# Moving the input normalisation of an attention and feed-forward kernel from VectorE to ScalarE and GpSimd, with a new instruction order on all engines

## The chip, the cores and the metric

The kernel runs on one core of one Trainium2 chip, in one launch. The metric is device time in microseconds (us). A core has engines that run side by side, each with its own in-order instruction stream: TensorE (PE in the profile), VectorE (DVE), ScalarE (ACT), GpSimd (POOL) and SyncE (SP), which here only issues DMA transfers. They wait for each other through semaphores.

## The reference, cut to what matters

The input is 16 sequences of 512 rows by 256 columns. Attention has 16 heads of 16 columns; its softmax is a second-order polynomial, so that sums over keys can be taken once per sequence. A layer normalisation stands ahead of attention, another behind it, and the same around a feed-forward product whose input and weight are rounded to a six-bit grid in blocks of 32.

```python
def _layernorm(x, axis=-1, eps=1e-05):
    m = jnp.mean(x, axis=axis, keepdims=True)
    v = jnp.var(x, axis=axis, keepdims=True)
    return (x - m) / jnp.sqrt(v + eps)

# inside attention
h = (x - mu) * jax.lax.rsqrt(var + EPS) * ln_w + ln_b
q = h @ w_q
kv = h @ w_kv
# heads, rotary embedding, then
def _taylor_softmax(x):
    t = 1.0 + x + 0.5 * x * x
    return t / jnp.sum(t, axis=-1, keepdims=True)

x = x + _layernorm(attention(_layernorm(x)))
x = x + _layernorm(ffn(_layernorm(x)))
```

The change touches the first normalisation, `(x - mean) * rstd`, whose result is named `z`.

## The kernel before

The 16 x 512 rows are 64 tiles of 128 rows, four tiles per sequence. Every tile goes through the same stages, and the tiles overlap deeply: while tile 30 is being normalised, the projections of tile 28, the attention of tile 21 or 22 and the feed-forward product of tile 13 are under way. The polynomial softmax makes attention two phases: `sum_features` adds up products of keys and values over the four tiles of a sequence (features `kf`, values `vp`, into the banks `ps_mt`), then, per quad of heads, `select` and `attend` apply these sums to the queries.

For each tile, in short:

- VectorE: `stats_x`, `moments_x` (mean and variance, `mv`), `normalise_x` (writes `z`), after the transpose `low_h` (`hT_l`), after the projection `rope_sin`, `rope_cos`, `rope_add` (rotary embedding into `kf`), `extend_k`, `products_0` and `products_1` (feature products), `normalise_attention` (`att`), `add_attention` (`xs`), and the quantisation and closing steps of the feed-forward part (`amax`, `sc`, `inv`, `y`, `xd`, `xdT_l`, `fb`, `fin`).
- GpSimd: `add_x` and `rstd_x` (the inverse root `rs_x` of the variance, by a power), the same pair for the three other normalisations, `half_turn`, `products_2`, `low_q`, `low_attention`.
- TensorE: `turn_z` (transposes `z` into `ps_tr`), `project_kq` (six products of 512 columns into `ps_qk`), `project_v` (six of 256 into `ps_tr`), `turn_q`, five `select` products of 512 columns into `ps_f`, `attend` (eight products of 32 output rows and 512 columns), `sum_features` (16 of 153 columns), `project_out` and `ffn` (six of 256 each, into `ps_w`) and `turn_ffn_input`.
- ScalarE: `high_h` (`hT_h`, the high part of the transposed `z`), `square` five times (from `ps_f` into `feat`), `copy_quad` (`osb`), `copy_q`, `copy_v`, `high_q`, `square_k`, `centre`, the three squares for the variances, and further copies out of the accumulation banks.

The bank `ps_tr` serves `turn_z`, `turn_ffn_input`, `project_v` and `turn_q` one after the other; each waits until ScalarE, or ScalarE and then VectorE, has read what the last one left. So `turn_z`, `high_h`, `low_h` is a chain across three engines that closes before the next use.

The order of the work on each engine is a table of numbers, `ORDER`: for each stage, the slots at which its tiles stand in the engine's stream (a list of first slots, a cycle of four tiles with a pitch, and a list of last slots). `every_step` walks through the slots and emits the stage that stands there. `IDLE` names slots at which TensorE runs products whose result nobody reads (`idle_products`, two per entry `fill`; `warm_up` is twelve of them at the start). In the kernel before, `IDLE` is empty.

The normalisation that is moved, in the kernel before (line 1476 and on):

```python
def normalise_x(t):
    dve.wait_ge(rstd["x"], t.n)
    wait(dve, zT_done, t.n - 2)
    dve.tensor_scalar(z[:, t.two, 0:D - 1], xa[:, t.par, t.tile, 0:D - 1], mv[:, t.two, 0:1], rs["x"][:, t.two:t.two + 1],
                      ALU.subtract, ALU.mult).then_inc(z_ready, 1)
```

At the start of the program, before tiles can flow, the projection weights are folded with the layer norm's weights (`fold_kq`, `fold_v` on TensorE), split into a high and a low part (`wkqv_h` on ScalarE, `wkqv_l` on VectorE), and VectorE and ScalarE work out the angles of the rotary embedding and the rounding of the feed-forward weight.

Of the kernel before, what the change touches and what calls it, by code (L numbers as in the profile page):

```python
# [6 lines left out]
ALU = mybir.AluOpType  # L7
# [6 lines left out]
P = 128  # L14
D = 256
# [35 lines left out]
        "attend": ((43, 54, 65, 76, 90, 101, 114, 127, 140, 154, 168, 183, 198,), (25, 39, 53, 69,), (474, 489, 503,  # L51
            517, 533, 547, 561, 574, 591, 605, 619, 632, 643, 662, 676, 690, 706, 720, 734, 748, 763, 778, 791, 807,
            822, 841, 852, 863, 871, 884, 895, 911, 921,)),
        "ffn": ((143, 157, 173, 187, 204,), (145, 159, 173, 189,), (464, 480, 494, 508, 522, 539, 553, 565, 581, 597,
            611, 625, 640, 656, 670, 684, 698, 714, 727, 742, 757, 772, 787, 799, 813, 829, 842, 855, 872, 877, 885,
            896, 906, 913, 922, 928, 934, 937, 940, 943, 945, 947,)),
        "fold_kq": ((2,), (), ()),
        "fold_v": ((3,), (), ()),
        "project_kq": ((4, 8, 12, 17, 22, 28, 39, 50, 61, 73, 86, 97, 110, 122, 136, 150, 164, 176,), (-69, -55, -39,
            -25,), (526, 541, 555, 568, 584, 599, 613, 627, 637, 653, 667, 681, 695, 711, 729, 741, 754, 768, 785, 800,  # L60
            814, 830, 846,)),
        "project_out": ((108, 120, 132, 148, 161, 178, 194, 211, 225, 240, 255, 267, 281, 298, 311, 327, 341, 354,
            369,), (109, 124, 139, 153,), (531, 545, 559, 572, 589, 603, 617, 631, 648, 660, 674, 688, 701, 718, 731,
            746, 762, 776, 792, 804, 820, 834, 848, 859, 866, 880, 889, 900, 910, 918, 923, 929, 933, 936, 941,)),
        "project_v": ((5, 7, 13, 18, 23, 26, 37, 49, 62, 71, 84, 96, 107, 118, 135, 149, 163, 174, 188, 203, 215, 229,
            245,), (-74, -60, -44, -30,), (493, 507, 521, 537, 551, 567, 580, 595, 609, 623, 638, 654, 669, 683, 696,
            712, 724, 739, 752, 771, 784, 798, 815, 831, 847,)),
        "rest_matrix": ((29, 75, 128, 185, 242, 300,), (9,), (527, 585, 644, 705, 764, 821, 876,)),
# [1764 lines left out]
```

## Time and profile before

| | |
|---|---|
| time, median of 3 runs | 645.48 us (644.69 to 649.01) |
| time of the profiled execution | 651.11 us |
| its span, first to last instruction | 648.8 us |
| busy: TensorE | 615.9 us, 95% |
| busy: VectorE | 594.8 us, 92% |
| busy: ScalarE | 530.0 us, 82% |
| busy: GpSimd | 449.3 us, 69% |
| mean granted TensorE clock | 0.985 |

The profile comes from one execution. Its page gives busy time by engine, the costliest groups of instructions (line, engine, output <- input, count, busy time, mean duration, idle time just before them), and what ended the waits. A timeline lists instructions in order of time; equal neighbours are merged into one row. A matmul's end is modelled and overlaps the start of the next one, so that a busy TensorE need not be TensorE at its peak; the distance from one start to the next tells more. A matmul on 32-bit data is recorded as two, so "x8" is four such products. The other engines too show instructions that overlap by about a tenth of a microsecond when they follow directly.

### The profile page before, as it was taken

To read this page: it belongs to the slowest core of one execution; us is meant where nothing else is said; L and a number is where in the kernel's file an instruction comes from. 1 tells how busy PE (TensorE), PEld (TensorE's weight loads), DVE (VectorE), ACT (ScalarE), POOL (GpSimd) and SP (SyncE) were. 2 spreads that over 40 slices of the span, in tenths; PEclk is the share of its full clock that TensorE was granted. 3 is DMA by queue.
4 is the path that set the end of the run, shared out by engine and by line. 5 is a ranking of instruction groups with operands and counts; after the bars stand their busy time and mean duration, and the time that the engine had idled before them with its cause. 6 is when DMAs were issued, how large, how long until landed. Compare 5 with 4: busy or idle time off the path is not lost. (4 is left out here: it accounts for less than half of the span.)

```text
span 648.8 us, 20724 instructions
## 1 busy us (share of the span) xinstructions
PE 615.9 (95%) x6620; PEld 457.7 (71%) x6620; DVE 594.8 (92%) x1489; ACT 530.0 (82%) x1448; POOL 449.3 (69%) x785
## 2 busy tenths in 40 slices
PE   6889999999999999999999999999999999999974
PEld 5666667676776776777777777767777766788763
DVE  5799899899899989999999999989999999987796
ACT  4347788888788897989888888978888888999973
POOL 3475466677777878788777867767877777765464
PEclk9699999999999999999999999999999999999996
DMA  7101031222223232232323232223223212230201
GB/s 245 34 2 42 20 76 30 72 63 65 50 72 88 70 91 68 75 84 67 62 67 83 77 86 73 69 57 101 60 68 92 76 39 41 68 91 18 68 26 49
DMA packets 52362, 43.51 MB, mean 67 GB/s; under 512 B 7201, under 2 KB 48545, under 8 KB 52257
## 3 DMA queue, kind: packets, MB, share of 16 engines
q1 hardware_dynamic: 51440, 41.42, 24.1%
q8 instruction: 55, 0.90, 0.6%
q10 hardware_dynamic: 816, 0.79, 0.4%
q14 instruction: 51, 0.41, 0.2%
HBM read 18.65 MB, written 8.39 MB: 42 GB/s over the span
## 5 line engine op out<-in xcount | busy, mean ns | idle before, releaser
L1168 ACT ACTIVATE feat<-ps_f 128x512 f32<-128x512 f32 x256 | 144.4, 599 | 4.9 <-PE ps_f L852 4.3
L691 DVE TENSOR_TENSOR kf<-kf 128x896 f32<-128x896 f32 (+1 forms) x128 | 131.2, 1027 | 1.8
L852 PE MATMUL ps_f<-qT,selr 128*128 128x512 f32 x320 | 122.1, 435 | 1.8 <-ACT qT L1236 1.3
L691 POOL TENSOR_TENSOR kf<-kf 128x224 f32<-128x224 f32 x64 | 76.5, 1195 | 13.3 <-DVE kf L1515 11.1
L1015 PEld LDWEIGHTS ps_mt<-kf,vp 128*32 128x32 f32 x2048 | 64.1, 110 | 30.0 <-issue 28.3
L1015 PE MATMUL ps_mt<-kf,vp 128*32 128x153 f32 x2048 | 79.7, 296 | 0.6 <-DVE kf L691 0.6
L1725 POOL TENSOR_TENSOR qsp<-kf,qsp 128x256 fp32r<-128x256 f32 x64 | 58.6, 916 | 9.8 <-ACT qsp L1259 9.6
L852 PEld LDWEIGHTS ps_f<-qT,selr 128*128 128x128 f32 x320 | 52.8, 190 | 15.2 <-issue 11.0
L913 PE MATMUL ps_o<-feat,main 120*32 120x512 f32 x448 | 59.7, 604 | 0.0
L916 PE MATMUL ps_o<-feat,rm 128*32 128x512 f32 x448 | 58.6, 593 | 0.0
L788 PE MATMUL ps_qk<-wkqv_h,hT_l 128*128 128x512 f32 x128 | 52.4, 409 | 3.3 <-DVE wkqv_l L1425 3.3
L1737 POOL TENSOR_TENSOR kf<-kf 128x128 f32<-128x128 f32 x64 | 37.4, 584 | 25.9 <-DVE kf L1508 25.8
L1750 POOL TENSOR_TENSOR ve_x<-mv,epsx 128x1 f32<-128x1 f32 x64 | 22.9, 358 | 45.5 <-DVE mv L1474 44.5
L1253 ACT ACTIVATE osb<-ps_o,cb 128x512 f32<-128x512 f32 x56 | 38.5, 687 | 15.9 <-PE ps_o L916 15.0
L789 PE MATMUL ps_qk<-wkqv_l,hT_h 128*128 128x512 f32 x128 | 51.0, 399 | 0.0
L1744 POOL TENSOR_TENSOR attT_l<-att,attT_h 128x256 fp32r<-128x256 f32 x56 | 42.7, 763 | 11.7 <-ACT attT_h L1208 10.9
L1236 ACT ACTIVATE qT<-ps_tr 128x512 fp32r<-128x512 f32 x64 | 38.2, 596 | 14.1 <-PE ps_tr L876 13.3
L1499 DVE TENSOR_TENSOR t<-ps_qk,sinT 128x512 f32<-128x512 f32 x64 | 43.4, 678 | 5.1 <-PE ps_qk L791 4.8
L1750 POOL TENSOR_TENSOR ve_s<-var_s,epst 128x1 f32<-128x1 f32 x64 | 21.8, 341 | 37.4 <-issue 32.4
L1170 ACT ACTIVATE feat<-ps_f,small 128x512 f32<-128x512 f32 x64 | 44.3, 692 | 2.7 <-PE ps_f L852 1.1
L1490 DVE TENSOR_TENSOR t<-ps_qk,cosT 128x512 f32<-128x512 f32 x64 | 43.1, 674 | 2.0 <-PE ps_qk L791 1.6
L1754 POOL TENSOR_TENSOR rs_x<-ve_x,mhalf 128x1 f32<-128x1 f32 x64 | 43.3, 676 | 2.4
(199 smaller groups left out, 1885.2 us busy)
## 6 DMA issues: line engine op xcount, KB each, us to landing
xc<-L_attn_x SPq DMA_DIRECT2D x16, 512.0 KB, 4.5
result<-fin SPq DMA_DIRECT2D x64, 128.0 KB, 2.0
xa<-L_attn_x SPq DMA_DIRECT2D x15, 512.0 KB, 4.1
heads_out<-osb SPq DMA_DIRECT2D x224, 32.0 KB, 2.0
shares<-sums SPq DMA_DIRECT2D x112, 64.0 KB
sums<-osb SPq DMA_DIRECT2D x224, 2.0 KB
wkqv<-L_attn_w_kv ACTq DMA_DIRECT2D x2, 256.0 KB, 4.9
xa<-L_attn_x SPq DMA_DIRECT2D x1, 384.0 KB, 6.2
```

What stands on the lines that cost most here:

```text
L691: return eng.tensor_tensor(dims(row, F_MAIN, [[FW, heads], [HD, NR - 1], [1, HD]]), dims(row, F_LIN, [[FW, heads], [0, NR - 1], [1, HD]]), ...
L788: pe.matmul(out_, xl(c), wh(c), start=c == 0, stop=False)
L789: pe.matmul(out_, xh(c), wl(c), start=False, stop=False)
L852: pe.matmul(ps_f[i % 2][:, :], selr[:, i], queries, start=True, stop=True).then_inc(sel_done, 1)
L913: pe.matmul(ps_o[VW * h:VW * (h + 1), :], main[0:NP, par, quad, VW * h:VW * (h + 1)], feat[0:NP, p2, h], start=True, stop=False, skip_grou ...
L916: mm = pe.matmul(ps_o[VW * h:VW * (h + 1), :], rm[:, par, quad, VW * h:VW * (h + 1)], feat[:, p2, HQ], start=False, stop=True, skip_group_ ...
L1015: mm = pe.matmul(ps_mt[qd // 2][VW * h:VW * (h + 1), (qd % 2) * NF:(qd % 2 + 1) * NF], vp[:, s2, qd * HQ + h], kf[:, s2, qd * HQ + h, 0:NF ...
L1168: act.activation(feat[:, p2, i], ps_f[i % 2][:, :], ACT.Square).then_inc(squared, 1)
L1170: act.activation(feat[:, p2, i], ps_f[0][:, :], ACT.Square, bias=rest_add).then_inc(squared, 1)
L1499: dve.tensor_tensor(dims(t2[:], 0, [[HD, 2 * H], [2, 8], [1, 2]]), dims(ps_qk[:, :], 1, [[HD, 2 * H], [2, 8], [-1, 2]]), sin, ALU.mult).th ...
L1725: pool.tensor_tensor(dims(qsp[:, p2], HQ * HD, [[2 * HQ * HD, NQ], [HD, HQ], [1, HD]]), dims(kf[:, p2, 0, 0:1], F_Q, [[HQ * FW, NQ], [FW, ...
L1750: pool.tensor_tensor(ve[c][:, t.two:t.two + 1], variance, floor, ALU.add).then_inc(pool_step[c], 1)
```

## The change

The normalised input is no longer written by VectorE as `(x - mean) * rstd`, but by ScalarE as `x * rstd + shift`, where `shift = -mean * rstd` is one number per row, worked out by GpSimd in a new step `shift_x` (tile `centre_x`). Two waits guard the double-buffered small tiles: `rstd_x` and `shift_x` wait until ScalarE has written `z` two tiles back, and `moments_x` until the shift two tiles back is there. `constant` and `rest_terms`, once per sequence, are each cut into two stages with the same instructions, which the order may place apart. All slots of `ORDER` are new, and `IDLE["fill"]` has twelve entries, so 24 products whose result nobody reads are added to the first 20 slots of TensorE.

```diff
-IDLE = {"fill": (), "drain": ()}
+IDLE = {"fill": (1, 1, 4, 4, 4, 7, 9, 10, 14, 14, 19, 19,), "drain": ()}
...
+        centre_x = sb("centre_x", [P, 2])
...
+            def normalise_x(t):
+                act.wait_ge(x_centred, t.n)
+                wait(act, zT_done, t.n - 2)
+                act.activation(z[:, t.two, 0:D - 1], xa[:, t.par, t.tile, 0:D - 1], ACT.Identity,
+                               bias=centre_x[:, t.two:t.two + 1], scale=rs["x"][:, t.two:t.two + 1]).then_inc(z_ready, 1)
...
             def moments_x(t):
                 dve.wait_ge(stats, t.n)
                 wait(dve, z_ready, t.n - 2)
+                wait(dve, x_centred, t.n - 2)
                 dve.bn_aggr(mv[:, t.two], st[:, t.two]).then_inc(means, 1)
-
-            def normalise_x(t):
-                dve.wait_ge(rstd["x"], t.n)
-                wait(dve, zT_done, t.n - 2)
-                dve.tensor_scalar(z[:, t.two, 0:D - 1], xa[:, t.par, t.tile, 0:D - 1], mv[:, t.two, 0:1], rs["x"][:, t.two:t.two + 1],
-                                  ALU.subtract, ALU.mult).then_inc(z_ready, 1)
...
+            def sum_linear(t):
+
+                dve.wait_ge(mt_copied, t.seq + 1)
+                wait(dve, cb_ready, t.seq)
+                dve.tensor_reduce(lins[:], mts[:, :, F_LIN:NF], AX.X, ALU.add).then_inc(lins_done, 1)
+
             def constant(t):
-
-                dve.wait_ge(mt_copied, t.seq + 1)
-                dve.tensor_reduce(lins[:], mts[:, :, F_LIN:NF], AX.X, ALU.add).then_inc(lins_done, 1)
                 dve.wait_ge(lins_done, t.seq + 1)
...
             def rstd_x(t):
+                wait(pool, z_ready, t.n - 2)
                 inverse_root("x", t)
+
+            def shift_x(t):
+
+                pool.wait_ge(rstd["x"], t.n)
+                wait(pool, z_ready, t.n - 2)
+                pool.tensor_scalar(centre_x[:, t.two:t.two + 1], mv[:, t.two, 0:1], rs["x"][:, t.two:t.two + 1], -1.0,
+                                   ALU.mult, ALU.mult).then_inc(x_centred, 1)
```

VectorE, in the middle of the program, behind `low_h` of the 29th tile. Before:

```order
L1575 TENSOR_TENSOR hT_l<-ps_tr,hT_h 128x256
L1604 TENSOR_SCALAR sc<-amax 128x8
L1499 TENSOR_TENSOR t<-ps_qk,sinT 128x512
L1608 RECIPROCAL inv<-sc 128x8
L1612 SCALAR_TENSOR_TENSOR y<-c,inv 128x256
L1582 TENSOR_TENSOR xdT_l<-ps_tr,xdT_h 128x256
L1479 TENSOR_SCALAR z<-xa,mv,rs_x 128x255
L1593 SCALAR_TENSOR_TENSOR xs,ssum<-ps_w,rs_y,xc 128x256
L1620 SCALAR_TENSOR_TENSOR xd<-y,rs_s,sc 128x256
L1508 TENSOR_TENSOR kf<-t 128x2x16x16
```

And now, behind the same instruction:

```order
L1586 TENSOR_TENSOR hT_l<-ps_tr,hT_h 128x256
L1521 COPY kf<-kf 128x16x7
L696 TENSOR_TENSOR kf<-kf 128x6x112
L1604 SCALAR_TENSOR_TENSOR xs,ssum<-ps_w,rs_y,xc 128x256
L696 TENSOR_TENSOR kf<-kf 128x8x112
L1593 TENSOR_TENSOR xdT_l<-ps_tr,xdT_h 128x256
L1610 TENSOR_REDUCE amax<-c 128x8
L1481 BN_STATS st<-xa 128x6
L1569 TENSOR_TENSOR att<-heads_out,shares 128x256
L1505 TENSOR_TENSOR t<-ps_qk,sinT 128x512
```

The instruction that wrote `z` is gone, and the feature products now stand directly behind `low_h`, with the rotary embedding later.

ScalarE, in the same round, now (the row that writes `z` is new; `feat` are the squares, `ps_f` their input, `qT` is `copy_q`):

```order
L1173 ACTIVATE feat<-ps_f 128x512 x2
L1232 ACTIVATE vp<-ps_tr 128x16x16
L1175 ACTIVATE feat<-ps_f,small 128x512
L1218 ACTIVATE z<-xa,centre_x,rs_x 128x255
L1247 ACTIVATE qT<-ps_tr 128x4x128
L1213 ACTIVATE attT_h<-att 128x256
L1173 ACTIVATE feat<-ps_f 128x512
```

The same place before:

```order
L1168 ACTIVATE feat<-ps_f 128x512
L1170 ACTIVATE feat<-ps_f,small 128x512
L1236 ACTIVATE qT<-ps_tr 128x4x128
L1208 ACTIVATE attT_h<-att 128x256
L1216 ACTIVATE hT_h<-ps_tr 128x256
```

Behind the new instruction stand `copy_q`, the high part of attention and the first square of the next quad.

TensorE at the start of the program, now (`one` is the operand of the idle products, L892 is `turn_z`, L806 and L816 the folding of the weights, L793 the first projection):

```order
L831 MATMUL ps_o<-one 128x128 x16
L892 MATMUL ps_tr<-small,z 128x128 x2
L806 MATMUL ps_f<-wkqv,wa 128x512 x2
L806 MATMUL ps_w<-wkqv,wa 128x512 x2
L816 MATMUL ps_f<-wkqv,wa 128x256 x4
L831 MATMUL ps_o<-one 128x128 x6
L892 MATMUL ps_tr<-small,z 128x128 x2
L793 MATMUL ps_qk<-wkqv_h,hT_l 128x512
```

And before:

```order
L826 MATMUL ps_o<-one 128x128 x12
L887 MATMUL ps_tr<-small,z 128x128 x2
L801 MATMUL ps_f<-wkqv,wa 128x512 x2
L801 MATMUL ps_w<-wkqv,wa 128x512 x2
L811 MATMUL ps_f<-wkqv,wa 128x256 x4
L788 MATMUL ps_qk<-wkqv_h,hT_l 128x512
```

Four idle products are added ahead of the folding, six behind it, and the transpose of the second tile now stands ahead of the first projection. The fourteen others stand in pairs and fours between the projections of the first tiles.

## Rows read from the trace of the kernel before

**Rows 1.** The page: span, and its part 1, busy us by engine.

```profile
span 648.8 us, 20724 instructions
PE 615.9 (95%) x6620; PEld 457.7 (71%) x6620; DVE 594.8 (92%) x1489; ACT 530.0 (82%) x1448; POOL 449.3 (69%) x785
```

**Rows 2.** Busy us (instructions) by stretch, then granted clock, DMA share, GB/s.

```profile
260.00:540.00 280.00, 278.05 (x2930) 204.79 (x2929) 271.00 (x676) 243.16 (x664) 213.21 (x364) 1.00 0.28 73
620.00:649.00 29.00, 16.74 (x107) 13.72 (x105) 21.69 (x73) 16.00 (x57) 15.02 (x38) 0.83 0.12 42
```

**Rows 3.** Timeline of VectorE (start us, us, engine, line): `low_h` of tiles 29, 62.

```profile
243.35 0.41 DVE L1575 TENSOR_TENSOR hT_l<-ps_tr,hT_h 128x256 fp32r<-128x256 f32 x1
...
548.46 0.43 DVE L1575 TENSOR_TENSOR hT_l<-ps_tr,hT_h 128x256 fp32r<-128x256 f32 x1 [0.23 <-ACT hT_h L1216]
```

**Rows 4.** Timeline of TensorE, part of one round.

```profile
299.77 1.06 PE L913 MATMUL ps_o<-feat,main 120*32 120x512 f32 x8
300.65 1.04 PE L916 MATMUL ps_o<-feat,rm 128*32 128x512 f32 x8
301.51 1.22 PE L1015 MATMUL ps_mt<-kf,vp 128*32 128x153 f32 x32
302.66 0.50 PE L852 MATMUL ps_f<-qT,selr 128*128 128x512 f32 x1
303.00 0.28 PE L788 MATMUL ps_tr<-wkqv_h,hT_l 128*128 128x256 f32 x1
...
303.72 0.28 PE L788 MATMUL ps_w<-wdt_h,xdT_l 128*128 128x256 f32 x1
...
304.44 0.39 PE L852 MATMUL ps_f<-qT,selr 128*128 128x512 f32 x1
304.67 0.56 PE L876 MATMUL ps_tr<-identr,qsp 128*128 128x128 f32 x4
305.06 0.44 PE L852 MATMUL ps_f<-qT,selr 128*128 128x512 f32 x1
```

**Rows 5.** Groups of instructions: count, busy us, mean ns, idle before, releaser.

```profile
L1750 POOL TENSOR_TENSOR ve_x<-mv,epsx 128x1 f32<-128x1 f32 x64 | 22.9, 358 | 45.5 <-DVE mv L1474 44.5
L1279 ACT ACTIVATE c<-xs,ssum 128x256 f32<-128x256 f32 x64 | 32.6, 509 | 5.4 <-DVE xs L1593 5.0
L1479 DVE TENSOR_SCALAR z<-xa,mv,rs_x 128x255 f32<-128x255 f32 x64 | 29.7, 465 | 1.2 <-POOL rs_x L1754 0.9
```

**Rows 6.** Timeline of VectorE: the write of `z` and what directly follows.

```profile
309.13 0.40 DVE L1479 TENSOR_SCALAR z<-xa,mv,rs_x 128x255 f32<-128x255 f32 x1
...
309.45 0.41 DVE L1582 TENSOR_TENSOR xdT_l<-ps_tr,xdT_h 128x256 fp32r<-128x256 f32 x1
```

**Rows 7.** Timeline of ScalarE: `high_q`, no per-row operand, and its follower.

```profile
54.08 0.42 ACT L1259 ACTIVATE qsp<-kf 128x256 fp32r<-128x256 f32 x1
54.39 0.43 ACT L1264 ACTIVATE kf<-kf 128x256 f32<-128x256 f32 x1
```

**Rows 8.** Timeline of TensorE: the first product of the first four `project_kq`.

```profile
16.64 0.47 PE L788 MATMUL ps_qk<-wkqv_h,hT_l 128*128 128x512 f32 x1 [3.29 <-DVE wkqv_l L1425]
...
23.54 0.63 PE L788 MATMUL ps_qk<-wkqv_h,hT_l 128*128 128x512 f32 x1
...
28.98 0.45 PE L788 MATMUL ps_qk<-wkqv_h,hT_l 128*128 128x512 f32 x1
...
34.36 0.45 PE L788 MATMUL ps_qk<-wkqv_h,hT_l 128*128 128x512 f32 x1
```

**Rows 9.** By stretch, columns as in rows 2: the early stretches of TensorE's clock.

```profile
12.00:16.00 4.00, 1.35 (x7) 0.84 (x5) 3.79 (x13) 2.37 (x7) 1.72 (x6) 1.00 0.58 185
...
18.00:19.00 1.00, 1.00 (x5) 0.90 (x4) 0.67 (x2) 0.00 (x0) 0.00 (x0) 0.50 0.00 0
...
28.00:29.00 1.00, 1.00 (x21) 0.75 (x13) 1.00 (x5) 0.00 (x0) 0.00 (x0) 0.99 0.00 0
```

**Rows 10.** Groups: the 12 idle products at the start, in 24 records.

```profile
L826 PE MATMUL ps_o<-one 128*128 128x128 f32 x24 | 5.2, 412 | 2.8 <-POOL rm L1694 2.8
```

**Rows 11.** Waits: who, for whom, us in total, times, longest.

```profile
DVE att L1558 <- DMA shares<-sums: 9.1, 8, 1.9
```

More of the change, by code:

```diff
@@ L50 @@
     "tensor": (58, {
[L51 to L56, printed above, removed]
+        "attend": ((42, 54, 65, 79, 88, 102, 112, 123, 140, 154, 168, 183,), (24, 38, 52, 68,), (547, 562, 575, 586,
+            604, 619, 633, 648, 662, 676, 690, 705, 720, 734, 747, 764, 778, 793, 807, 818, 837, 850, 859, 871, 886,
+            905, 915, 922,)),
@@ new lines @@
+        "turn_ffn_weight": ((75,), (), ()),
+        "turn_q": ((10, 16, 21, 27, 40, 48, 60, 70, 83, 94, 109, 122, 130, 149, 163, 177, 193, 207, 221, 235, 251, 265,
+            279, 292,), (-39, -25, -11, 3,), (584, 599, 613, 627, 641, 657, 671, 685, 699, 715, 729, 742, 756, 773, 787,
+            801, 816, 831, 844, 856, 869,)),
+        "turn_quads": ((879, 880, 893, 903, 909, 918, 926, 931,), (), ()),
+        "turn_sums": ((26, 74, 118,), (4,), (578, 642, 700, 758, 814, 867,)),
+        "turn_z": ((1, 4, 7, 12, 18, 23, 29, 43, 55, 66, 78, 89, 101, 114, 126, 137, 153, 167, 182, 197, 211, 225, 240,
+            255, 269, 283, 298, 313, 327, 341, 355,), (-79, -65, -50, -35,), (587, 603, 617, 631, 644, 661, 675, 689,
+            704, 719, 733, 745, 760, 777, 791, 805, 819, 835,)),
@@ new lines @@
+        "cast_selection": ((3,), (), ()),
+        "centre": ((153, 167, 181, 203, 227, 245, 262, 278, 302, 313, 334, 352, 369, 385, 408, 424, 445, 461, 483, 498,
+            518, 541, 556, 573, 594, 613, 630, 648, 672, 689, 709, 725, 744, 766, 780, 802, 821, 836, 859, 876, 897,
+            915, 935, 954, 969, 991, 1010, 1024, 1046, 1067, 1083, 1098, 1109, 1122, 1138, 1149, 1160, 1172, 1180, 1187,
+            1192, 1198, 1204, 1209,), (), ()),
+        "centre_bias": ((130,), (), ()),
+        "copy_ffn_weight": ((96,), (), ()),
@@ new lines @@
+        "high_h": ((5, 12, 18, 23, 32, 36, 44, 60, 75, 87, 97, 113, 127, 147, 161, 174, 194, 212, 230, 248, 268, 288,
+            308, 325, 343, 361, 380, 399, 418, 438, 456, 475, 492, 511, 531, 550, 569, 587, 606, 625, 644, 663, 681,
+            701, 719, 738, 757, 776, 794, 814, 830, 852, 869, 888, 906, 925, 943, 961, 979, 1000, 1019, 1037, 1058,
+            1076,), (), ()),
+        "high_kq": ((7,), (), ()),
+        "high_q": ((19, 24, 29, 38, 48, 56, 70, 82, 93, 109, 114, 129, 143, 166, 180, 198, 216, 240, 258, 273, 298, 315,
+            330, 349, 370, 388, 403, 423, 440, 462, 481, 500, 519, 540, 555, 576, 595, 616, 632, 651, 665, 687, 703,
+            721, 741, 764, 784, 799, 826, 846, 857, 875, 901, 919, 936, 952, 975, 997, 1011, 1030, 1051, 1070, 1088,
+            1104,), (), ()),
@@ L1313, in step @@
                 setup(n, "centre_bias", centre_bias)
+                each(n, "normalise_x", normalise_x)
                 each(n, "high_h", high_h)
@@ L1530, in constant, with scale_terms @@
                                          ALU.mult, ALU.add).then_inc(cb_ready, 1)
-            def rest_terms(t):
+            def scale_terms(t):
                 dve.wait_ge(mt_copied, t.seq + 1)
@@ L1537, in rest_terms @@
                 dve.tensor_scalar(rest[:, :, HD:VW], mts[:, :, F_LIN:NF], ALPHA / 2, None, ALU.mult).then_inc(lins_scaled, 1)
+            def rest_terms(t):
                 dve.wait_ge(lins_scaled, t.seq + 1)
@@ L1638, in step @@
             def step(n):
+                once(n, "sum_linear", sum_linear)
                 once(n, "constant", constant)
@@ L1658, in step @@
                 each(n, "from_grid", from_grid)
-                each(n, "normalise_x", normalise_x)
                 setup(n, "weight_cast_high", weight_cast_high)
@@ L1662, in step @@
                 setup(n, "weight_scales", weight_scales)
+                once(n, "scale_terms", scale_terms)
                 once(n, "rest_terms", rest_terms)
@@ L1788, in step @@
                 each(n, "rstd_x", rstd_x)
+                each(n, "shift_x", shift_x)
                 setup(n, "scale_ln", scale_ln)
```

441 lines of the change are left out of this document (213 added, 228 removed), and 94 rows, old and new, of the table ORDER.

## The prediction

> **What bounds the kernel now.** I began with the busy shares of the page [rows 1]. Three engines lie between 82% and 95%, so the shares alone name no bound. I then asked for busy time by stretch, because start, middle and end do different work. In the middle [rows 2], TensorE is busy 278.05 of 280 us, VectorE 271.00 (96.8%), ScalarE 243.16 (86.8%) and GpSimd 213.21 (76%). In the last 29 us nothing is normalised any more, and VectorE is busy 21.69 us.
>
> TensorE's 99% is to be mistrusted, since ends of matmuls are modelled. The timeline tells what it needs [rows 4]: `attend` and `sum_features` take 0.88, 0.86 and 1.15 us from start to start; six products of 256 columns take 0.72 (303.00 to 303.72, and again to 304.44); a `select` 0.23 where nothing is waited for (304.44 to 304.67); `turn_q` 0.39. A tile has one `attend`, one `sum_features` (together 2.89), three groups of six at 256 columns (2.16), one of six at twice the width (1.44), five selects (1.15), one `turn_q` (0.39) and two transposes of two blocks (about half a `turn_q` each, 0.4): 8.4 us. Once per sequence come `turn_sums` (the size of `turn_q`) and twenty small products (I take 0.7), a quarter of it per tile, 0.3. So TensorE needs 8.7 us per tile.
>
> The time per tile is read from `low_h`, which runs once per tile [rows 3]: 33 tiles from 243.35 to 548.46 are 305.1 us, 9.25 us each. By the shares of rows 2, VectorE is busy 0.968 x 9.25 = 8.95 us of it, ScalarE 8.03, GpSimd 7.04. So VectorE is the nearest to the bound, by 0.25 us over TensorE, and the round is 0.30 us longer than VectorE's own work. That last part is what in-order engines lose on each other.
>
> **What the change costs and brings.**
>
> *VectorE loses `z`.* 64 instructions of mean 465 ns [rows 5] leave. They overlap their neighbours: the follower starts 0.32 us after `z` (309.13 to 309.45, [rows 6]). I take 0.31 us per tile, 20 us in all. VectorE then needs 8.64 us per tile.
>
> *ScalarE gains `z`.* No row shows it with two per-row operands. `high_q`, 256 wide and without any, lasts 0.42 us and its follower starts 0.31 us after it [rows 7]; `centre`, with one, has a mean of 509 ns [rows 5], so that one operand costs 0.09. With two I expect about 0.60 us of duration and 0.49 us from start to start; the bounds are 0.40 (one operand, overlapped) and 0.60 (nothing overlapped). ScalarE then needs 8.03 + 0.49 = 8.52 us per tile, 31 us more in all.
>
> *GpSimd gains `shift_x`.* One operation on 128x1; the nearest is `add_x`, 358 ns [rows 5]. I take 0.3 (0.2 to 0.4), so 7.04 + 0.3 = 7.3 us per tile, still 1.9 under the round. What hides it is that margin; what it lengthens is the chain variance, root, shift, `z`, transpose. The normalised tile is two tiles ahead of the projections, so it is hidden as long as the shift isn't queued behind a late `products_2`, which stands ahead of it on GpSimd. If `z` is late on ScalarE, `copy_q`, the high part of attention and the next quad's squares are queued behind it, and TensorE's selects wait for those.
>
> *The added waits* look two tiles back and cost nothing. The parts cut out of `constant` and `rest_terms` are the same instructions.
>
> *The new order.* Before, `turn_z` is followed by two selects and `project_out` until `ps_tr` is needed again, 0.46 + 0.72 = 1.2 us of cover for `high_h` and `low_h`; now it is followed by `attend` and `sum_features`, 2.9 us. I see one place where the order gains and none where it plainly loses, but give it no term of its own. The wait of VectorE for the inverse sums, 9.1 us in 8 times [rows 11], may move in either direction; in the new order `invert_sums` and the first `att` that needs it stand somewhat closer together.
>
> *Steady part.* After the change TensorE needs 8.7, VectorE 8.64 and ScalarE 8.52 us per tile: three engines within 0.2 us. The round was 0.30 us above the busiest one; with three so near each other it should be a little more, and I choose 0.34: 9.04 us, a gain of 0.21 per tile. The bounds are 0.31 (all that VectorE loses) and 0 (a round 0.55 above the busiest). Between 60 and 560 us, where this rate holds, about 54 tiles pass: 54 x 0.21 = 11.3 us (0 to 17).
>
> *Clock and idle products.* TensorE waits 3.29 us for the low part of the weights before the first `project_kq` [rows 8], and in the stretch around that it is busy 1.35 of 4 us. After that the granted clock falls to 0.50 (1.2 GHz) and is back at 0.99 in the stretch from 28 us [rows 9]. The first four tiles start at 16.64, 23.54, 28.98 and 34.36 us [rows 8]: 6.9 and 5.4 us apart at the half clock, against 5.4 and later about 5 where VectorE sets the pace. At the full clock throughout, the first two intervals would shrink by at most (6.9 - 5.1) + (5.4 - 5.1) = 2.1 us. I take 2.0.
>
> By the Trainium skill ("TensorE: Matmul & The Clock Gate", "What's actually happening") the throttled clock is the default and activity releases it, so idle products in the gap should hold it. The trace agrees so far as the clock fell after the gap.
>
> The idle products' own price: twelve take 5.2 us [rows 10], 0.43 each, and half at the full clock. The six behind the folding (1.3 to 2.6 us) fit into the wait of 3.29; the four ahead of it delay the folding by 0.9 to 1.7 us, which the same wait hides, because VectorE and not the folding is late there. The fourteen others (3 us) stand in gaps of the first tiles. If VectorE were not late, they would cost up to 4 us. `turn_z` of tile 2 now stands ahead of the first projection, behind a longer chain; I take it at 0, up to 0.5 lost.
>
> *Tail.* The last 29 us have no `z`; 0.
>
> *The sum:* 11.3 + 2.0 = 13.3 us. On the profiled execution this is 651.1 - 13.3 = 637.8. The median of the runs before is 645.48, 5.6 below that execution, so I forecast 645.5 - 13.3 = 632.2, rounded to 632.
>
> **The rivals.**
>
> *All of it, or more.* VectorE was the only bound and the new order keeps the others clear: 54 x 0.31 = 17 us, 2 from the clock, and 2 to 5 of the 9.1 us of waits for the inverse sums: about 623. For it: 96.8% of VectorE. Against: TensorE's 8.7 us.
>
> *TensorE takes over at once.* Its needs are nearer to the round than I count (its busy share, 99%, says so), and VectorE only waits longer for `ps_qk` and `ps_tr`. Then only the clock is left: 643.
>
> *ScalarE becomes the bound; slower.* It is idle 9.25 - 8.03 = 1.22 us per tile today, most of it waits for TensorE's results, in order. The point from which it decides is 9.25 - 8.52 = 0.73 us: if the waits per tile stay above that, the round grows. At 1.0 it is 9.52, 54 x 0.27 = 15 us, less 2: 658. For it: the new row stands ahead of `copy_q` and the squares, and depends on GpSimd. Against: an engine that becomes the bound waits less, since its inputs are ready by then.
>
> The Trainium skill speaks for this rival ("ScalarE: Activation LUTs", "Rules for kernel authors"): plain additions and multiplications belong on VectorE. The trace agrees on the price, 0.31 us per row there against my 0.49 on ScalarE.
>
> *The clock isn't held* (the idle products leave a gap or only delay the first tiles): 2 us less, 634; this lies in my range and changes no sign.
>
> **How the numbers follow.** A measurement of this kernel tells about 1% (6.5 us) from no change. My forecast, 632 (626 to 639), has 0.50; all of it or more, 0.17; TensorE at once, 0.22; ScalarE slower, 0.11. Faster by over 1% (below 639.0) takes the first two and a little of the third less what the first loses above 639: 0.68. Within 1%: 0.21. Slower: 0.11. The range leaves out the slower case and the far end of the best one: 621 to 645.
>
> **What would show it.** Right: `low_h` about 9.0 us apart in the middle; VectorE's share down to 95% or 96%, ScalarE's up to 93% or 95%; `z` on ScalarE near 0.60 us; granted clock near 1.00 from 12 to 30 us; the second `project_kq` 5 to 5.5 us after the first. Wrong: rounds of 9.25 us with VectorE idle 0.5 us in each, waiting for TensorE (the second rival); ScalarE rows with long waits for GpSimd's shift, or squares late and selects waiting for them (the third); a clock of 0.5 in the same place. A steady round as predicted but a longer end would mean that the new order lost in the tail, where I counted nothing.

## The result and the profile after

The changed kernel takes 656.43 us (median of 4 runs, 652.53 to 659.29), beside 646.91 us (4 runs, 644.69 to 649.01) for the kernel before: a ratio of 1.014, 95% interval 1.008 to 1.021. It is slower by 1.4%, where 632 us was forecast. The profiled execution took 652.53 us, against 651.11 before, so its trace shows less than the whole difference. Below, a gain or loss of a kernel is always the ratio of its runs; where in the program it lies is read from spans.

The page after, its span and busy times (answers to [rows 1]):

```profile
span 650.9 us, 21023 instructions
PE 618.7 (95%) x6668; PEld 462.8 (71%) x6668; DVE 579.6 (89%) x1425; ACT 551.8 (85%) x1512; POOL 468.6 (72%) x849
```

VectorE lost 15.2 us of work, ScalarE gained 21.8 and GpSimd 19.3. So the work did move, and nothing came of it. The middle stretch, with the columns of [rows 2]:

```profile
260.00:540.00 280.00, 273.24 (x2839) 202.71 (x2832) 255.38 (x633) 249.06 (x680) 223.37 (x393) 0.99 0.28 72
```

Every engine has time to spare here: TensorE 6.8 us, VectorE 24.6, ScalarE 30.9. Before, TensorE had 2.0 us and VectorE 9.0. The two engines nearest to the bound both idle more than before, so the work that VectorE lost isn't what holds them now; ScalarE, which got the work, still idles most of the three. That points to waits, possibly for something that is not an engine's work. The instruction list of `low_h` (once per tile) tells where time goes: count, duration in ns (least, median, greatest), and the first and last start in us, for three stretches of the changed kernel. The first ends and the second begins with tile 29.

```profile
L1586 DVE TENSOR_TENSOR hT_l<-ps_tr,hT_h x21: 409/420/425, 62.5 to 239.8; 128x256 fp32r<-128x256 f32 x21
L1586 DVE TENSOR_TENSOR hT_l<-ps_tr,hT_h x34: 389/417/426, 239.8 to 548.1; 128x256 fp32r<-128x256 f32 x34
L1586 DVE TENSOR_TENSOR hT_l<-ps_tr,hT_h x2: 417/418/419, 562.3 to 570.1; 128x256 fp32r<-128x256 f32 x2
```

The same of the kernel before, for the two stretches that [rows 3] don't give:

```profile
L1575 DVE TENSOR_TENSOR hT_l<-ps_tr,hT_h x20: 353/418/425, 65.5 to 233.0; 128x256 fp32r<-128x256 f32 x20
L1575 DVE TENSOR_TENSOR hT_l<-ps_tr,hT_h x2: 412/418/425, 557.5 to 567.3; 128x256 fp32r<-128x256 f32 x2
```

The table puts these starts together (us), with e1, an experiment below:

| `low_h` of | before | after | e1 |
|---|---|---|---|
| tile 9 | 65.5 | 62.5 | 62.8 |
| tile 29 | 243.35 | 239.8 | 239.6 |
| tile 62 | 548.46 | 548.1 | 539.4 |
| tile 64 | 567.3 | 570.1 | 558.8 |
| end of span | 648.8 | 650.9 | 639.9 |

After the change the first 29 tiles are 3.5 us ahead. Then 33 tiles take 308.3 us, 9.34 each, where they took 9.25 before and 9.04 were forecast, and the lead is gone. Two more tiles take 22.0 us instead of 18.8.

The waits of VectorE after (who, for whom, us in total, times, longest), and the longest one of ScalarE. The first line has no counterpart before, where `fin` waited only for GpSimd's `rs_f`:

```profile
DVE fin L1646 <- DMA result<-fin: 12.2, 6, 4.3
ACT c L1290 <- DVE xs L1604: 15.8, 20, 3.3
ACT z L1218 <- POOL centre_x L1794: 5.0, 4, 2.3
```

VectorE waits 12.2 us, six times, for a *store*: `fin` has two buffers, and its third writer needs the first buffer's transfer to have landed. The longest case, first SyncE's queue (start, time of issuing, transfers merged), then VectorE and ScalarE:

```profile
459.90 2.25 SPq L761 DMA_DIRECT2D sums<-osb  x4
462.19 2.45 SPq L765 DMA_DIRECT2D heads_out<-osb  x4
464.69 0.58 SPq L734 DMA_DIRECT2D xa<-L_attn_x  x1
465.32 2.23 SPq L761 DMA_DIRECT2D sums<-osb  x4
467.59 3.14 SPq L765 DMA_DIRECT2D heads_out<-osb  x4
470.78 0.58 SPq L739 DMA_DIRECT2D xc<-L_attn_x  x1
471.40 5.30 SPq L750 DMA_DIRECT2D result<-fin  x3
```

VectorE in the same time (start, duration; the wait in brackets):

```profile
458.43 0.48 DVE L1646 SCALAR_TENSOR_TENSOR fin<-fb,rs_f,xs 128x256 f32<-128x256 f32 x1
...
471.12 0.41 DVE L1586 TENSOR_TENSOR hT_l<-ps_tr,hT_h 128x256 fp32r<-128x256 f32 x1
475.87 0.48 DVE L1646 SCALAR_TENSOR_TENSOR fin<-fb,rs_f,xs 128x256 f32<-128x256 f32 x1 [4.33 <-DMA result<-fin]
```

And ScalarE, behind it:

```profile
478.35 0.51 ACT L1290 ACTIVATE c<-xs,ssum 128x256 f32<-128x256 f32 x1 [3.28 <-DVE xs L1604]
```

SyncE issues its transfers one after the other, about 0.6 us each: a quad's eight (four `sums`, four `heads_out`) take it 4.7 us. Between 459.90 and 471.40 it issues, without a gap, two quads and two input loads, and only then the stores. The store of the `fin` written at 458.43 is not even issued for 13 us. VectorE stands still for 4.33 us at the third `fin`, and ScalarE's `c` waits behind it for the `xs` that VectorE has not reached. TensorE runs out of work too: it is busy 2.01 us of the four from 476 us, and its granted clock (third column from the end) falls to 0.74 and 0.83. Before and in e1 it is 1.00 from 60 to 620 us.

```profile
476.00:480.00 4.00, 2.01 (x8) 1.94 (x9) 4.00 (x12) 1.37 (x4) 0.39 (x2) 0.74 0.11 35
480.00:484.00 4.00, 4.00 (x29) 3.40 (x31) 2.95 (x9) 3.21 (x10) 2.24 (x4) 0.83 0.14 33
```

The same queue before has a store between every two quads in the middle of the program:

```profile
280.28 2.24 SPq L756 DMA_DIRECT2D sums<-osb  x4
282.56 2.45 SPq L760 DMA_DIRECT2D heads_out<-osb  x4
285.06 0.59 SPq L745 DMA_DIRECT2D result<-fin  x1
285.69 0.44 SPq L734 DMA_DIRECT2D xc<-L_attn_x  x1
286.17 2.25 SPq L756 DMA_DIRECT2D sums<-osb  x4
288.46 2.43 SPq L760 DMA_DIRECT2D heads_out<-osb  x4
290.94 0.58 SPq L745 DMA_DIRECT2D result<-fin  x1
```

In the changed kernel the wait of VectorE begins at 471.54, just after the store is issued. So the 13 us in the queue have used up what two buffers cover, and the 4.33 us are the landing of the store. The three stores issued from 471.40 on took, from issue to landing (us):

```profile
DMA to landing us min/median/max: 1.7/4.1/4.4
```

It is the same in all six waits: each begins after its store was issued. Four of the six stores go out directly behind the load of an input (512 KB) and take 4.2 to 4.5 us to land; the other two take 2.0 and 2.6, and the median of all stores is 2.4. In the lines of before above, the store stands ahead of the load. So a second cause may lie in the same queue: had those four stores landed in 2.4 us, about 7 of the 12.2 us of waits would be gone (an estimate from these numbers). No run here moves only the loads behind the stores, so how the loss divides between the two isn't shown.

So the theory: the new order of *SyncE* puts stores behind pairs of quads, two result buffers don't cover that, and the loss of this exceeds the gain of the moved normalisation. The rivals: ScalarE is late with `z` and the squares; the new order of the other engines loses by itself.

### The profile page after: what moved, and what is told of

Same layout as the page of the kernel before. It is cut to its first block, busy times and chain, and to the rows that moved or that the text cites. A ratio compares the mean times of both kernels' runs of the same rounds, so it can differ in the third digit from the quotient of the medians.

```text
span 650.9 us, 21023 instructions
## 1 busy us (share of the span) xinstructions
PE 618.7 (95%) x6668; PEld 462.8 (71%) x6668; DVE 579.6 (89%) x1425; ACT 551.8 (85%) x1512; POOL 468.6 (72%) x849
## 4 chain that ended last, share of the span: by engine, by line
PE 67%; DVE 9%; issue 8%; POOL 6%; DMA 4%; ACT 3%; SPq 2%; DVEq 0%; POOLq 0%; ACTq 0%
PE ps_f L857 10%; PE ps_mt L1020 8%; PE ps_o L918 6%; PE ps_o L921 6%; PE ps_w L793 4%; PE ps_qk L793 4%; PE ps_qk L796 3%; PE ps_qk L794 3%; PE ps_w L796 3%; PE ps_w L794 3%; PE ps_tr L881 3%; PE ps_tr L793 2%; PE ps_tr L871 2%; PE ps_tr L892 2%; PE ps_tr L796 2%
## 5 line engine op out<-in xcount | busy, mean ns | idle before, releaser
L1173 ACT ACTIVATE feat<-ps_f 128x512 f32<-128x512 f32 x256 | 146.6, 599 | 3.3 <-PE ps_f L857 3.0
L1737 POOL TENSOR_TENSOR qsp<-kf,qsp 128x256 fp32r<-128x256 f32 x64 | 54.0, 843 | 20.1 <-ACT qsp L1270 20.0
L696 POOL TENSOR_TENSOR kf<-kf 128x224 f32<-128x224 f32 x64 | 63.7, 995 | 5.9 <-DVE kf L1521 5.8
L1756 POOL TENSOR_TENSOR attT_l<-att,attT_h 128x256 fp32r<-128x256 f32 x56 | 47.7, 851 | 13.5 <-ACT attT_h L1213 13.3
L1749 POOL TENSOR_TENSOR kf<-kf 128x128 f32<-128x128 f32 x64 | 39.0, 609 | 18.0 <-DVE kf L1514 17.9
L793 PE MATMUL ps_qk<-wkqv_h,hT_l 128*128 128x512 f32 x128 | 51.6, 403 | 0.0
L1514 DVE TENSOR_TENSOR kf<-t 128x512 f32<-128x512 f32 x64 | 45.4, 709 | 1.8 <-PE ps_mt L1020 1.0
L1290 ACT ACTIVATE c<-xs,ssum 128x256 f32<-128x256 f32 x64 | 32.8, 513 | 16.4 <-DVE xs L1604 15.8
L1646 DVE SCALAR_TENSOR_TENSOR fin<-fb,rs_f,xs 128x256 f32<-128x256 f32 x64 | 33.1, 517 | 14.7 <-DMA result<-fin 12.2
L1762 POOL TENSOR_TENSOR ve_y<-var_y,epst 128x1 f32<-128x1 f32 x64 | 22.1, 345 | 33.2 <-ACT squares_y L1281 32.0
```

The source lines that it names most:

```text
L696: return eng.tensor_tensor(dims(row, F_MAIN, [[FW, heads], [HD, NR - 1], [1, HD]]), dims(row, F_LIN, [[FW, heads], [0, NR - 1], [1, HD]]), ...
L793: pe.matmul(out_, xl(c), wh(c), start=c == 0, stop=False)
L1173: act.activation(feat[:, p2, i], ps_f[i % 2][:, :], ACT.Square).then_inc(squared, 1)
L1514: dve.tensor_tensor(dims(kf[:, t.two, 0, 0:1], F_LIN, [[F_Q - F_LIN, 2], [FW, H], [1, HD]]), t1[:].rearrange("p (a h d) -> p a h d", a=2, ...
L1737: pool.tensor_tensor(dims(qsp[:, p2], HQ * HD, [[2 * HQ * HD, NQ], [HD, HQ], [1, HD]]), dims(kf[:, p2, 0, 0:1], F_Q, [[HQ * FW, NQ], [FW, ...
L1756: pool.tensor_tensor(attT_l[:, t.two].rearrange("p c n -> p (c n)"), att[:, t.two], attT_h[:, t.two].rearrange("p c n -> p (c n)").bitcast ...
```

## The experiments

Each ratio is to the kernel before on the same chip. The experiments ran on three chips (e1 to e4, e5 to e8, e9 to e12), on which the kernel before had medians of 647.63, 647.57 and 647.09 us, so their medians may be compared to about half a microsecond beyond the noise. The names: "the move" is `z` on ScalarE with its shift on GpSimd, "the order" the new tables.

**Four result buffers (e1).** A scratch tile that is free by then gives two more buffers; nothing else changes in the changed kernel.

```diff
-        stored = [sem("stored0"), sem("stored1")]
+        stored = [sem("stored%d" % i) for i in range(4)]
...
+        def final(t):
+            return fin[:, t.two] if t.four < 2 else wq2[:, t.two]
...
-                wait(dve, stored[t.two], 16 * ((t.n - 1) // 2))
-                dve.scalar_tensor_tensor(fin[:, t.two], fb[:, t.two], rs["f"][:, t.two:t.two + 1], xs[:, t.four],
+                wait(dve, stored[t.four], 16 * ((t.n - 1) // 4))
+                dve.scalar_tensor_tensor(final(t), fb[:, t.two], rs["f"][:, t.two:t.two + 1], xs[:, t.four],
```

> The changed kernel, but the closing tile fin has four buffers instead of two (two of them in a scratch tile of the setup that is free by then), so that VectorE need not wait for the store of two tiles back. Store theory: the changed kernel loses to stores that stand behind other transfers in SyncE's queue (12.2 us of VectorE's waits in six places, up to 4.3 us each, none in the kernel before); then these waits vanish and the ratio to the kernel before falls from 1.014 to about 0.995, some 12 us less. ScalarE theory: the moved instruction and its place are the cause, the waits for stores only fill time that would be lost anyway; then the ratio stays within 1.010 to 1.018. Order theory (the new order on TensorE, VectorE and GpSimd): as the ScalarE theory.

Measured: 641.53 us, ratio 0.990 (0.987 to 0.994). The middle stretch of e1:

```profile
260.00:540.00 280.00, 279.38 (x2915) 207.89 (x2908) 264.70 (x653) 256.55 (x702) 229.55 (x404) 1.00 0.29 73
```

Its `low_h` from tile 29 to tile 62:

```profile
L1590 DVE TENSOR_TENSOR hT_l<-ps_tr,hT_h x34: 390/417/426, 239.6 to 539.4; 128x256 fp32r<-128x256 f32 x34
```

No wait for a store is left, and 33 tiles take 299.8 us, 9.08 each. The buffers give back 14.9 us of medians and 11.0 us between the spans of the two profiled executions (650.9 and 639.9), beside 12.2 us of waits. The two rival theories expected 1.010 to 1.018 and fall: ScalarE and the orders are the same as in the changed kernel, and the loss is gone. Without the store wait the change is a gain of 1%.

**The same buffers in the kernel before (e11).**

> The kernel before with four result buffers instead of two (as in e1) and nothing else: control for e1. In the kernel before no instruction waits for a store, so the store theory expects 1.00 within 0.2%. If the buffers themselves bring something in any order (rival), the ratio is 0.99 or less, and e1 said nothing on the changed kernel.

Measured: 648.84 us, ratio 1.003 (1.001 to 1.005). The buffers bring nothing where no store is late; at 0.3% slower they lie a little outside the 0.2% expected. So none of e1's gain is theirs by themselves.

**The old order of SyncE alone (e2).** The changed kernel with the table `"sync"` of the kernel before.

> The changed kernel with the transfer order (SyncE's table) of the kernel before, all other engines as changed. Store theory: stores are spread again, fin waits less than 4 us in all, and the ratio falls to about 1.000 or below. ScalarE and order theories: no more than 0.3% better than the changed kernel (1.014), perhaps worse since this table was made for other places of the copies.

Measured: 655.21 us, ratio 1.011 (1.008 to 1.015). `fin` no longer waits for stores, but a wait of the same kind takes its place:

```profile
DVE sums L1553 <- DMA sums<-osb: 13.7, 6, 5.0
```

VectorE's inversion of the sums now waits 13.7 us for a quad's transfers. The time came out where the rival theories had it (at most 0.3% better than 1.014), so this run alone decides nothing for the stores. Its trace says that the loss is again a wait for SyncE's queue: SyncE's stream has to fit the other engines' orders as a whole, and the old one doesn't fit the new ones.

**Stores moved ahead in SyncE's new order (e6).** Two buffers as in the changed kernel; the stores of tiles 15 to 41 stand ahead of the second quad of a pair.

> The changed kernel with two buffers for fin, where in SyncE's order the stores of tiles 15 to 41 that stood behind the second of two quads are put ahead of it, so that less is queued ahead of a store. Store theory: VectorE's waits for stores shrink from 12.2 us to under 5 us, ratio 0.992 to 1.003. If a second wait for the queue appears instead (the sums of a quad now come later), the ratio stays at 1.010 to 1.014 with waits of invert_sums for its transfer.

Measured: 651.42 us, ratio 1.007 (1.004 to 1.009). Some waits remain:

```profile
DVE fin L1642 <- DMA result<-fin: 7.2, 4, 2.5
```

Both numbers miss what was expected (under 5 us of waits, a ratio of 1.003 at most). 12.2 us became 7.2, and the median is 5.0 us below that of the changed kernel, a third of what e1 gives back. The direction is that of the store theory. That the two differences are equal is luck: the four runs of the changed kernel alone spread over 6.8 us.

**Both cures (e12).** e6 with the four buffers of e1.

> The changed kernel with both cures: four result buffers (e1, 0.990) and the stores of the middle ahead of the second quad's transfers in SyncE's order (e6, 1.0065 with two buffers). With four buffers no store is waited for, so moving stores ahead can only delay the quads' transfers. Store theory: 0.990 to 0.995, not better than e1, and VectorE's waits for the gathered sums grow. Rival (SyncE's order costs something beyond the stores): below 0.988.

Measured: 641.06 us, ratio 0.991 (0.988 to 0.994), the same as e1. Once the buffers cover the delay, the place of the stores is worth nothing.

**The idle products alone (e4)**, `IDLE` of the changed kernel in the kernel before.

> The kernel before with the twelve entries of idle products added at the same slots, nothing else. Prediction's term: the clock stays at full speed from 12 to 30 us and 2 us are won, ratio 0.997. Rival: the products only delay the first tiles or the clock was not the limit there, ratio 1.000 to 1.004.

Measured: 646.31 us, ratio 0.998 (0.996 to 1.000). The granted clock (third column from the end), 0.72 and 0.50 before in these two stretches, is now full:

```profile
16.00:20.00 4.00, 3.21 (x18) 2.60 (x18) 3.91 (x11) 1.75 (x5) 0.78 (x3) 1.00 0.00 0
20.00:24.00 4.00, 3.51 (x26) 3.16 (x30) 3.86 (x8) 1.44 (x4) 3.88 (x5) 1.00 0.03 6
```

**e1 without the idle products (e8).**

> e1 (four buffers for fin) without the twelve entries of idle products. By e4 they are worth 0.2%: ratio about 0.993, and a granted clock of 0.5 somewhere between 15 and 30 us. Rival: e1's order leaves no long gap, so that the clock stays anyway: 0.990.

Measured: 642.68 us, ratio 0.993 (0.992 to 0.995), 1.2 us above e1 by the medians and 2.0 by the ratios. Here the clock falls again, to 0.76 and 0.81 in these stretches and to 0.50 from 19 to 21 us:

```profile
16.00:20.00 4.00, 2.48 (x8) 2.04 (x9) 1.85 (x5) 3.13 (x8) 2.05 (x6) 0.76 0.00 0
20.00:24.00 4.00, 3.38 (x15) 2.41 (x13) 3.50 (x6) 1.62 (x5) 1.50 (x2) 0.81 0.47 131
```

Both pairs say the same: the idle products hold the clock and are worth 1.2 to 2.0 us. How much is uncertain: the interval of e4 reaches nearly to nothing, and those of e8 and e1 overlap.

**The new order without the move (e5).** e1 with `z` back on VectorE, at a place that I chose (behind `products_0` of two tiles back, where the rows allow it).

> The changed kernel with four buffers for fin (as e1, ratio 0.990), but z written by VectorE again as in the kernel before (about three instructions behind low_h), no shift on GpSimd: new order and idle products without the move. If the move brings the 0.2 us per tile of the prediction, this is some 11 us slower than e1: ratio about 1.007. If e1's gain is the new order's and the move is worth nothing, ratio 0.988 to 0.993.

Measured: 659.32 us, ratio 1.019 (1.017 to 1.021). The middle stretch:

```profile
260.00:540.00 280.00, 273.77 (x2896) 200.91 (x2896) 268.94 (x666) 237.88 (x652) 212.16 (x358) 1.00 0.27 71
```

The group that writes `z` (before: [rows 5], 465 ns):

```profile
L1481 DVE TENSOR_SCALAR z<-xa,mv,rs_x 128x255 f32<-128x255 f32 x64 | 35.9, 561 | 0.5 <-POOL rs_x L1763 0.4
```

That is slower than either expectation had it. Against e1 the move is worth 17.8 us, 2.9%, in the new order. A tile takes 9.40 us here (32 tiles from 245.8 to 546.7) and 9.08 in e1. Part of that is `z` itself, which takes 561 ns in this place and not 465, so the place may not be the best one for it, and the new order was made for a stream without it. So the 1.9% belong to this placing; what the order would cost with the best place for `z` isn't shown.

**The move in the old order (e3).** The kernel before; `z` on ScalarE stands behind the fifth square, and the shift behind `rstd_x` on GpSimd.

> The kernel before with the normalisation moved and nothing else reordered: z is written by ScalarE right behind the fifth square of the quad under way (ahead of copy_q, where the changed kernel has it too), GpSimd works out the shift directly behind the root, the order of everything else and the empty list of idle products stay. Prediction's reasoning: VectorE was nearest to the bound, so 54 tiles x 0.2 us = 11 us less, ratio about 0.983. ScalarE theory: ScalarE's in-order waits plus 31 us of work make the round longer, ratio 1.01 to 1.03. Order and store theories: the move itself is worth something between 0 and -11 us, ratio 0.983 to 1.000.

Measured: 705.97 us, ratio 1.090 (1.087 to 1.094). Nine per cent slower, outside every range that I had named, with the same work on the same engines as in e1 (but for the idle products). Its waits:

```profile
DVE sums L1544 <- DMA sums<-osb: 36.3, 7, 6.6
SPq L728 <- ACT z L1212: 106.6, 9, 24.3
```

**`z` earlier in the old order (e7).** As e3, with `z` of most tiles behind `high_q` instead.

> As e3 (the kernel before with only the move), but z stands some six instructions earlier on ScalarE, behind high_q instead of behind the fifth square, for tiles 4 to 45. In e3 SyncE waited 106.6 us for z before it loaded the next sequence (56.6 in the kernel before), the quads' sums behind that load came late and VectorE waited 36.3 us for them. Queue theory: with z early again these waits are gone and the ratio falls from 1.090 to between 0.985 and 1.010. ScalarE theory (its in-order load is what costs): ratio stays above 1.05.

Measured: 709.20 us, ratio 1.096 (1.093 to 1.099), no better, where the ScalarE theory had it. But the edit did only part of what it was for. `z` now waits for its shift (18.6 us in 11), SyncE still waits 87.5 us for `z` (106.6 in e3), and VectorE 23.1 us for the gathered sums (36.3 in e3). So an earlier place on ScalarE is no cure; whether the queue is the cause, this run can't tell, since the waits that it was to remove were still there.

**Input loads later on SyncE (e9).** The lines on SyncE's wait in e3 point elsewhere. SyncE's queue in e3:

```profile
279.82 0.58 SPq L744 DMA_DIRECT2D result<-fin  x1
291.10 0.40 SPq L728 DMA_DIRECT2D xa<-L_attn_x  x1
291.55 2.24 SPq L755 DMA_DIRECT2D sums<-osb  x4
293.83 2.44 SPq L759 DMA_DIRECT2D heads_out<-osb  x4
```

The ScalarE instructions that it waited for:

```profile
285.55 0.70 ACT L1258 ACTIVATE osb<-ps_o,cb 128x512 f32<-128x512 f32 x1
...
290.47 0.61 ACT L1212 ACTIVATE z<-xa,centre_x,rs_x 128x255 f32<-128x255 f32 x1
```

And VectorE, which waits for the quad's transfers:

```profile
295.85 0.94 DVE L1544 RECIPROCAL sums<-sums 64x128 f32<-64x128 f32 x1 [6.28 <-DMA sums<-osb]
```

The load of the next sequence overwrites the input buffer, so it waits for the last `z` of an older one, written from 290.47 to 291.08. The quad whose `osb` was ready at 286.25 stands behind it in the queue and isn't issued until 291.55, and VectorE waits 6.28 us for it. In the kernel before, the load clears at 299.90 and the next quad is ready only at 302.45: `z` was early there, because VectorE wrote it earlier than ScalarE does. e9 is e3 with each such load behind the spreading of the inverse sums:

```diff
-        "load_stream": ((0, 1, 6, 11, 20, 32,), (-24,), (76, 87, 98, 108, 119,)),
+        "load_stream": ((0, 1, 6, 13, 23, 34, 44, 55, 66, 77, 88, 99, 111, 122,), (), ()),
```

(the quads and spreadings that it is moved past go one slot forward).

> The kernel before with only the normalisation moved to ScalarE and GpSimd (as in e3), and in SyncE's order each load of a sequence's input stands behind the spreading of the inverse sums instead of ahead of the fourth quad's transfers. In e3 the load at 291.10 us waited until z of 290.47 was written; SyncE had been free from 280.40, osb of the fourth quad was written at 286.25, and its transfers were issued only from 291.55. SyncE's queue theory: e3's waits of VectorE for the gathered sums (36.3 us in 7) fall below 10 us, the groups of four tiles fall from 46.2 us to under 41, and the ratio to before falls from 1.090 to 1.03 or less. Rival (z itself is late on ScalarE in the old order, and turn_z, project_kq and what follows it are late with it): the transfers leave earlier but the ratio stays at 1.07 to 1.09.

Measured: 664.50 us, ratio 1.028 (1.024 to 1.031). The waits for the gathered sums and of SyncE for `z`:

```profile
DVE sums L1542 <- DMA sums<-osb: 0.6, 2, 0.4
SPq L726 <- ACT z L1210: 46.8, 3, 24.3
```

This is what the queue theory expected, in the waits and in the ratio. The place of one kind of instruction in a queue that computes nothing is worth 41 us, about 70% of what the move costs in the old order.

That is more than the 35.7 us of waits for the sums that are gone. A part of the difference is TensorE's clock. In e3, behind the wait above (three stretches from 292 us; TensorE's busy time is the first number behind the length, the granted clock the third from the end):

```profile
292.00:296.00 4.00, 0.74 (x5) 0.30 (x3) 0.15 (x1) 1.09 (x4) 1.43 (x3) 1.00 0.51 150
296.00:300.00 4.00, 2.16 (x10) 0.69 (x14) 3.78 (x11) 1.46 (x4) 0.00 (x0) 0.60 0.25 48
300.00:304.00 4.00, 4.00 (x45) 1.88 (x38) 3.53 (x7) 2.08 (x7) 2.51 (x5) 0.55 0.39 86
```

TensorE is busy 0.74 of four microseconds, and then the clock is 0.60 and 0.55. From 60 to 600 us the mean is 0.97 in e3; in e9 it is 1.00 from 60 to 580 us. TensorE is busy 633.8 us in e3 and 619.7 in e9 with the same products. So a wait that empties TensorE is paid twice.

The rest of the loss, 2.8%, isn't settled; the weight loads of TensorE's `turn_z` wait 15.0 us in 17 times for `z` there, against 3.6 in 3 after the change, but no run took that away.

**The control (e10)**, the same edit of SyncE's order without the move.

> The kernel before, z still on VectorE, with the same edit of SyncE's order as in e9 and nothing else: control. SyncE waits 56.6 us in 7 times for z before a load in the kernel before; if that also holds up transfers which somebody waits for there, the time falls by 0.5% or more. I expect 0.99 to 1.00, since VectorE waits only little for the gathered sums in the kernel before. Rival (the order of SyncE is never late before the move): 1.00 within 0.2%.

Measured: 645.93 us, ratio 0.999 (0.997 to 1.001). The place of the load costs nothing while `z` is early.

| | old order | new order, four buffers |
|---|---|---|
| `z` on VectorE | 1 (e11: 1.003) | 1.019 (e5) |
| `z` on ScalarE | 1.090 (e3), 1.028 (e9) | 0.990 (e1) |

As placed here, the move and the order are each a loss alone and a gain together. The edits don't add up. `z` stands in e3, e5 and e9 at places that I chose, and a better place may cost less. No instruction of e3 or e9 waits for a store, so two buffers are enough in the column "old order".

## Why the prediction was wrong

**The failed step is "the new order": "I see one place where the order gains and none where it plainly loses, but give it no term of its own."** I had read the orders of TensorE, VectorE and ScalarE, and not SyncE's. The prediction doesn't name SyncE at all. The stores, their two buffers and the 4.7 us that a quad takes SyncE stood in no sentence. That term measured 14.9 us of loss by the medians of e1 and the changed kernel (15.7 by their ratios; the interval of the changed kernel alone is 4 us to either side). Result and forecast lie 24.2 us apart: 14.9 from the stores, 7.2 from a gain of 6.1 us in e1 instead of 13.3, and 2.1 because the kernel before had a median of 647.63 us beside e1 and not 645.48.

**VectorE was the nearest bound: borne out.** Taking `z` off it gains 2.9% in the new order (e5 to e1), with the reserve on e5's place for `z`. In e1 VectorE is busy 264.70 of 280 us, so 8.59 us of a round of 9.08; I had 8.64. The rounds of e1, 9.08 us, are close to the 9.04 that I forecast for the change. My 20 us for `z` in all lie between what the traces show: VectorE's busy time falls by 13.7 us in the old order (before to e3) and by 28.3 in the new one (e5 to e1).

**Where that rate holds: mis-sized.** I took 54 tiles at 0.21 us, 11.3 us. From tile 9 to tile 29 a tile took 8.89 us before and 8.84 in e1: a gain of 0.05. From 29 to 62 it is 0.17, 5.4 us in 33 tiles. The rate had been read between 243 and 548 us and was carried back to 60 us, where the rounds are shorter. The profiled execution of before was also one of its slower ones: e4, e10 and e11, all within 0.3% of before by their ratios, show 9.21, 9.20 and 9.19 us in the later stretch (e10: 303.7 us for 33 tiles). Against e10 the gain of e1 is 0.03 in the first stretch and 3.9 us in the 33 tiles. So the 7.2 us of missing gain come about half from the first 20 tiles (0.18 x 20 = 3.6) and half from the smaller rate in the others (6.9 - 3.9 = 3.0), with up to 0.8 from the clock. These shares are read from single traces.

**ScalarE's price: a little too high.** `z` has a median of 600 ns, as forecast (0.60). The Trainium skill ("ScalarE: Activation LUTs", "What ACT_TABLE_LOAD costs") gives 186 ns + 0.833 ns per element and 93 ns for each per-row operand, an estimate of 584 ns for 255 elements; the trace agrees, its least is 584. From start to start I had 0.49. What the move alone adds to ScalarE's busy time is read within one order: 29.2 us from before to e3, 0.46 per tile, and 25.1 from e5 to e1, 0.39. From before to after it is only 21.8, because the new order by itself takes 3.7 off (before to e5). ScalarE is busy 256.55 of 280 us in e1, 8.32 us per tile where I had 8.52. The rival "ScalarE becomes the bound" did not happen, though the time, 656, is almost that of its forecast, 658; that is luck: had it been so, four result buffers would not have brought 14.9 us back.

**GpSimd's shift: about right.** GpSimd's busy time grows by 19.3 us from before to after, 0.30 per tile as forecast; within one order it is 0.25 (before to e3) and 0.36 (e5 to e1). The operation itself has a median of 322 ns and, with some much longer ones, a mean of 496, above my 0.2 to 0.4. It is hidden in the new order: `z` waits 5.0 us for it in all. The groups of both after the change (count, busy us, mean ns, idle before):

```profile
L1218 ACT ACTIVATE z<-xa,centre_x,rs_x 128x255 f32<-128x255 f32 x64 | 38.6, 605 | 5.0 <-POOL centre_x L1794 5.0
L1794 POOL TENSOR_SCALAR centre_x<-mv,rs_x 128x1 f32<-128x1 f32 x64 | 31.7, 496 | 2.2
```

**Clock: right in place and sign.** The clock is 1.00 from 12 to 32 us after the change, and worth 1.2 to 2.0 us where I had 2.0. What I had no term for is the clock later on: after the longest store wait it is 0.74 for four microseconds.

**Tail: right.** I counted 0 for it. From `low_h` of tile 64 to the end of the span it takes 81.5 us before, 80.8 after and 81.1 in e1. The 3.2 us that the changed kernel loses between tiles 62 and 64 come earlier, with the last store wait, 2.06 us at 555.23; e1, without it, loses 0.6 there.

**TensorE as the next bound: likely, not shown.** In e1 its records fill 279.38 of 280 us, so the needs that I added up as 8.7 us are probably too low. In the chain of work that ended last, TensorE has 74% and VectorE 9% in e1, where in e5 they have 57% and 20%. So the rival "TensorE takes over at once" (643) may hold a part of the truth about e1's 641.5. That is argued from shares; no run took work from TensorE.

## What to carry to other kernels

When a change brings a new order for all engines, read the queue that only issues transfers first. Count its issue time between the write of each buffer and the transfer that frees it, add the time that the transfer takes to land, and compare that with the number of buffers. When an in-order queue holds a wait for something that has moved to another engine, ask what stands behind it: a load that can wait must not stand ahead of a transfer that is needed in a few microseconds. And judge an order only together with the work it was made for: here each half alone, as placed, loses.

## What was not expected of the hardware

A transfer costs SyncE 0.5 to 0.8 us to issue, and its size doesn't decide: the medians after the change are 528 ns for `sums<-osb` (2 KB), 588 for `heads_out<-osb` (32 KB), 777 for `shares<-sums` (64 KB), 486 for `result<-fin` (128 KB) and 581 for the load `xa` (512 KB). In e3 SyncE stood 106.6 us waiting for `z`, and the page's list of busy engines shows nothing of it. The Trainium skill ("DMA: Bandwidth & Descriptors", "Anatomy of one DMA — SWDGE (gpsimd) path") says that the transfer engines don't wait for semaphores and that the wait happens on the issuing sequencer ahead of dispatch. The section is about transfers issued from GpSimd; e3's load on SyncE agrees: it is issued at 291.10, when `z` has ended at 291.08, and nothing is issued between 280.40 and then.

The same store takes 2.0 us to land in one place and 4.5 in another, directly behind a load. And the same VectorE instruction on the same shapes, `z`, took 465 ns on average in one order and 561 in another. The medians hardly differ, 407 and 412 ns: 11 of the 64 took over 500 ns before and 30 in e5. Each of these long ones ran beside an instruction of GpSimd for at least 70% of its time, but so did some of the short ones. What lengthens them was not tried.
